# Summing the last states in pairs, and moving the convolution, the last product and the first statistics, in a four-stage block on one core

## The reference

```
x = x + attention(layernorm(x))   # RMS norm with norm_w gives xn; 16 heads of 16, causal softmax; returns xn + out @ Wo.T + bo
x = x + ffn(layernorm(x))         # base product + shared and 6 routed rank-16 adapters, top 2 of 6 by softmax of a router
x = x + ssm(layernorm(x))         # below
x = x + ffn(layernorm(x))         # the same weights again

xc    = silu(causal depthwise convolution of 4 taps + conv_b)
delta = softplus(xc @ Wd.T + bd);  B = xc @ Wb.T;  C = xc @ Wc.T        # 16 states n
h_n[t] = exp(A_n * delta[t]) * h_n[t-1] + delta[t] * xc[t] * B_n[t]
y[t]   = sum over n of h_n[t] * C_n[t]
return (y * sigmoid(x @ Wg.T + bg)) @ Wo.T + bo
```

## Time and profile before

| | |
|---|---|
| time, median of 3 runs | 2346.57 us (2340.99 to 2353.04) |
| the profiled execution's own time | 2343.07 us |
| its span, first to last instruction | 2341.3 us |
| mean granted clock of TensorE | 0.901 |
| TensorE busy | 1801.8 us, 77% |
| VectorE busy | 1820.6 us, 78% |
| ScalarE busy | 1292.8 us, 55% |
| GpSimd busy | 1061.9 us, 45% |
| accumulates y<-hc | 240 of 512 KB, median 6.1 us from issue to landing |
| loads of a row of B | 256 of 256 KB, median 3.7 us |
| load of one batch of x | 16 of 512 KB, median 5.3 us |

### The profile page before, as it was taken

One profiled execution on the slowest core, in us unless ns is written; L12 is line 12 of the kernel. 1 busy time (PEld: TensorE's weight loads), 2 busy tenths in 40 slices (PEclk: granted clock), 3 DMA queues, 4 the chain that ended last, 5 costly groups with the idle time before them and its releaser, 6 DMA issues. The chain is left out here.

```text
span 2341.3 us, 31537 instructions
## 1 busy us (share of the span) xinstructions
PE 1801.8 (77%) x10784; PEld 1088.8 (47%) x10784; DVE 1820.6 (78%) x2791; ACT 1292.8 (55%) x2258; POOL 1061.9 (45%) x672
## 2 busy tenths in 40 slices
PE   3789887878788787878888797878878797866433
PEld 1445444545364454536454454635445453534222
DVE  4444878879797888969797878979787887959693
ACT  1455656565756556565656556565655655554331
POOL 1010544636354545535464543545454553546461
PEclk8899899999999899999999899999999998986756
DMA  3211565747665665756566674766557574645462
GB/s 108 78 55 60 122 144 123 166 106 167 127 134 124 131 150 126 161 111 146 123 132 143 127 161 106 165 120 145 122 123 157 118 159 101 137 93 123 95 143 45
DMA packets 190370, 291.25 MB, mean 124 GB/s; under 512 B 34034, under 2 KB 126211, under 8 KB 190211
## 3 DMA queue, kind: packets, MB, share of 16 engines
q1 hardware_dynamic: 155650, 163.40, 28.5%
q0 software_dynamic: 34560, 125.84, 28.1%
HBM read 128.72 MB, written 34.08 MB: 70 GB/s over the span
## 5 line engine op out<-in xcount | busy, mean ns | idle before, releaser
L1174 POOL TENSOR_TENSOR inp<-u,b_all 128x1024 f32<-128x1024 f32 x256 | 608.0, 2375 | 638.8 <-DVE hc L1027 517.4
L1027 DVE TENSOR_TENSOR_SCAN hc<-dec,inp 128x1024 f32<-128x1024 f32 x256 | 644.0, 2516 | 4.1 <-ACT dec L796 3.0
L707 ACT ACTIVATE pt<-bank 128x512 f32<-128x512 f32 x640 | 382.8, 600 | 410.3 <-PE bank L340 406.6
L315 PE MATMUL bank<-sk,sq 96*128 96x512 bf16 (+3 forms) x1024 | 283.7, 316 | 204.8 <-DVE mall L914 64.5
L796 ACT ACTIVATE dec<-dt,a_neg 128x511 f32<-128x511 f32 x512 | 338.5, 721 | 72.6 <-DVE hc L1027 72.5
L1182 POOL DMA_DIRECT2D y<-hc x240 | 211.6, 882 | 316.8 <-DVE hc L1034 183.6
L1034 DVE TENSOR_TENSOR hc<-hc,bank 128x1024 f32<-128x1024 f32 x240 | 291.1, 1213 | 61.3 <-PE bank L486 60.0
L338 PE MATMUL bank<-sq,sk 98*128 98x512 bf16 (+3 forms) x1024 | 280.6, 313 | 29.9 <-DMA sq<-hlt 21.0
L912 DVE TENSOR_REDUCE mall<-bank 128x1 f32<-128x512 f32 x256 | 171.6, 670 | 111.2 <-PE bank L317 111.1
L315 PEld LDWEIGHTS bank<-sk,sq 96*128 96x128 bf16 x1024 | 102.6, 100 | 330.8 <-DVE mall L914 86.3
L914 DVE TENSOR_REDUCE mall<-bank 128x4 f32<-128x512 f32 x256 | 174.8, 683 | 37.9 <-PE bank L317 33.7
(11 more groups left out here) (148 smaller groups left out, 3186.5 us busy)
## 6 DMA issues: line engine op xcount, KB each, us to landing
y<-hc POOLq DMA_DIRECT2D x240, 512.0 KB, 6.1
b_all<-b_kept SPq DMA_DIRECT2D x256, 256.0 KB, 3.7
qk_parts<-parts SPq DMA_DIRECT2D x96, 256.0 KB, 2.5
sq<-qk_parts SPq DMA_DIRECT2D x384, 64.0 KB, 4.1
sk<-qk_parts SPq DMA_DIRECT2D x384, 64.0 KB, 4.3
X<-in_x SPq DMA_DIRECT2D x16, 512.0 KB, 5.3
out<-X SPq DMA_DIRECT2D x16, 512.0 KB, 4.5
sq<-hlt SPq DMA_DIRECT2D x256, 2.0 KB
```

The costliest lines, as they stand in the source:

```text
L315: mm(dst[:, o:o + n], sq[0:KS, slot, h, qb * P:(qb + 1) * P], sk[0:KS, slot, h, 0:n], start=True, stop=False)
L707: A(pt[:, n % PT, :], score_bank[unit % 2][:, :], ACT.Exp).then_inc(exp_done.sem, 1)
L1027: V.tensor_tensor_scan(h, d, v, 0.0, ALU.mult, ALU.add).then_inc(scan_done.sem, 1)
L1174: G.tensor_tensor(inp[:, n % 2, :, :], u[:, :, :], b_all[:, n % 2:n % 2 + 1, :].to_broadcast([P, C, T]), ALU.mult).then_inc(inp_ready.sem, 1)
```

## The change

- **Pairs.** For batches 14 and 15 (`PAIRED = NB - 2`), after the product of an even state n = 2, 4, ..., 14 VectorE adds the slot of n - 1 to that of n, and one DMA adds the sum to y. State 15 is added alone. These batches have 8 accumulates each instead of 15, counted by `pair_added`; a scan waits for `pair_done` where its slot held an odd state, and for `pair_added` where it held an even one.
- **Convolution ahead of the gates.** Both halves of the convolution are at (3, 0), in banks MA and MB, both gates at (3, 1), in the same banks.
- **Last product a position later.** `gate_y` goes from (0, 1) to (0, 2), behind the scan of that position; `ssm_out` from (0, 4) to (0, 5); adding to X from (0, 4) to (0, 5) and the statistics to (0, 6); `rsqrt` from (0, 4) to (0, 7); normalising from (0, 9) to (1, 0). `turn_xn` goes from (0, 6) to (0, 3), and `head_norm` from the end of position 4 to position 5, behind the maximum and ahead of the scan.
- **Three slots for B.** Load k goes into slot k % 3 and waits for the inp of k - 3; the first three loads of a batch are issued together at (3, 4).
- **Start.** The statistics of the first x come first on VectorE, behind one small memset; the other memsets and the fold into Wv go into `constants`; Wv moves from the first to the other weights. ScalarE does one small exp ahead of its loop and waits for the constants at q = -1.
- The router's scratch tile `over` is dropped; `diff` is overwritten.

```diff
+    PAIRED = NB - 2
-        b_all = sb("b_all", [P, 2, T])
+        b_all = sb("b_all", [P, 3, T])
-    N_FIRST, N_REST = 5, 21
+    N_FIRST, N_REST = 4, 22
...
+            def ssm_conv(f, c):
+                m = (MA, MB)[c]
+                pe.wait_ge(m.free, m.fill(("conv", f, c)))
...
             def ssm_gate(f, c):
+                m = (MA, MB)[c]
+                pe.wait_ge(m.free, m.fill(("gate", f, c)))
+                by_columns(m.tile, wg, xs_t[:, :, TAPS - 1:], c).then_inc(m.full, 1)
...
-                    if (r, p, j) == (0, 6, 0):
+                    if (r, p, j) == (0, 3, 0):
                         turn_xn(b + 1)
...
-                    elif r == 3 and p in (0, 1):
-                        if j == 0:
-                            ssm_gate(f, p)
-                        else:
-                            ssm_conv(f, p)
+                    elif (r, p) == (3, 0):
+                        ssm_conv(f, j)
+                    elif (r, p) == (3, 1):
+                        ssm_gate(f, j)
...
-                    if (r, p) == (0, 4):
+                    if (r, p) == (0, 5):
                         ssm_out(l, j)
...
+                    old_s, old_n = divmod(k - 3, NS)
+                    sp.wait_ge(inp_ready.sem, inp_ready.at(old_s, old_n + 1))
+                    if n < 3:
                         sp.wait_ge(b_stored.sem, b_stored.at(s))
+                    sp.dma_start(b_all[:, k % 3, :], b_kept[s, n][None, :].to_broadcast([P, T])
+                                 ).then_inc(b_loaded[k % 3].sem, 16)
...
-                    if (r, p, j) == (0, 9, 0):
+                    if (r, p, j) == (1, 0, 0):
                         normalise(l, KIND_L, X[:, l % XS, :, :], y_tok(l))
...
+            act.wait_ge(pool_const, 1)
+            A(ex[:, 0, 0:1], ident[:, 0:1], ACT.Exp)
...
-                if q == -3:
+                if q == -1:
                     act.wait_ge(dve_const, 1)
...
+                    if old_n == 0:
+                        dve.wait_ge(hc_done.sem, hc_done.at(old_s, 1))
+                    elif old_s < PAIRED:
                         dve.wait_ge(y_added.sem, y_added.at(old_s, old_n))
+                    elif old_n % 2 and old_n < NS - 1:
+                        dve.wait_ge(pair_done.sem, pair_done.at(old_s - PAIRED, old_n // 2 + 1))
                     else:
+                        dve.wait_ge(pair_added.sem, pair_added.at(old_s - PAIRED, (old_n + 1) // 2))
...
+                    if s >= PAIRED and n and n % 2 == 0:
+                        dve.wait_ge(hc_done.sem, hc_done.at(s, n + 1))
+                        V.tensor_tensor(hc[:, k % HC, :, :], hc[:, k % HC, :, :], hc[:, (k - 1) % HC, :, :],
+                                        ALU.add).then_inc(pair_done.sem, 1)
...
-                    if (r, p) == (0, 1):
+                    if (r, p) == (0, 2):
                         gate_y(l)
-                    elif (r, p) == (0, 4):
+                    elif (r, p) == (0, 5):
                         add_to_x(l, ("x3",), (MA, MB))
+                    elif (r, p) == (0, 6):
                         moments(l, KIND_L, 1.0, 1e-5)
...
             V.memset(half[:, :], -0.5)
+            dve.wait_ge(x_loaded.sem, x_loaded.at(0))
+            moments(0, KIND_Q, 1.0 + 1e-6, 1e-5 * 1e-6)
             dve.wait_ge(pool_const, 1)
...
+                    if p == 5 and 0 <= q - 1 < NQ:
+                        head_norm(q - 1)
                     if p in STEP_AT:
                         scan(k + STEP_AT[p])
                     if p in PRODUCT_AT:
                         product(k + PRODUCT_AT[p])
-                    if p == 4 and 0 <= q - 1 < NQ:
-                        head_norm(q - 1)
...
+            def add_pair(s, n):
+                if n % 2 == 0:
+                    pool.wait_ge(pair_done.sem, pair_done.at(s - PAIRED, n // 2))
+                else:
+                    pool.wait_ge(hc_done.sem, hc_done.at(s))
+                if n > 2:
+                    pool.wait_ge(pair_added.sem, pair_added.at(s - PAIRED, (n - 1) // 2))
+                pool.dma_start(y[:, s % 2, :, :], hc[:, (NS * s + n) % HC, :, :],
+                               accum_op=ALU.add).then_inc(pair_added.sem, 16)
...
-                    elif (r, p) == (0, 4) and has(b - 3):
+                    elif (r, p) == (0, 7) and has(b - 3):
                         rsqrt(b - 3, KIND_L)
```

More of the change, by code:

```diff
@@ L245, in hybrid_block @@
         b_stored = tally("b_stored", 1, 16)
-        b_loaded = [tally(f"b_loaded{i}", NS // 2, 16) for i in range(2)]
+        b_loaded = [tally(f"b_loaded{i}", 1, 16) for i in range(3)]
         c_ready = tally("c_spread", NS)
@@ L448, in ssm_turn @@
                     turn(tok_f, m.tile, c).then_inc(m.full, 1)
-            def ssm_gate(f, c):
[L451 to L461, removed]
+            def ssm_conv(f, c):
+                m = (MA, MB)[c]
+                pe.wait_ge(m.free, m.fill(("conv", f, c)))
+                for k in range(TAPS):
+                    last = mm(m.tile[:, :], taps[:, c, k, :], xs_t[:, c, k:k + T], start=(k == 0),
+                              stop=(k == TAPS - 1))
+                last.then_inc(m.full, 1)
+            def ssm_gate(f, c):
+                m = (MA, MB)[c]
+                pe.wait_ge(m.free, m.fill(("gate", f, c)))
+                by_columns(m.tile, wg, xs_t[:, :, TAPS - 1:], c).then_inc(m.full, 1)
             def ssm_bc(f):
@@ L686, in _ @@
                         store_b(b - 1)
-                        load_b(NS * (b - 1))
-                        load_b(NS * (b - 1) + 1)
+                        for n in range(3):
+                            load_b(NS * (b - 1) + n)
                     if (r, p) == (3, 9) and has(b + 1):
                         store_parts(b + 1, 1)
-                    if (r, p) == (3, 9) and has(b - 1):
-                        load_b(NS * (b - 1) + 2)
             sp.wait_ge(x_stored.sem, x_stored.at(NB - 1))
@@ L757, in sigmoid_gate @@
             def sigmoid_gate(f, c):
-                act.wait_ge(MA.full, MA.at("gate", f, c))
-                A(gate[:, f % 2, c, :], MA.tile[:, :], ACT.Tanh, bias=bg_c[:, c:c + 1], scale=0.5).then_inc(MA.free, 1)
+                m = (MA, MB)[c]
+                act.wait_ge(m.full, m.at("gate", f, c))
+                A(gate[:, f % 2, c, :], m.tile[:, :], ACT.Tanh, bias=bg_c[:, c:c + 1], scale=0.5).then_inc(m.free, 1)
             def convolved(f, c):
-                act.wait_ge(MB.full, MB.at("conv", f, c))
-                A(sp_t[:, c, :], MB.tile[:, :], ACT.Tanh, bias=cb[:, c:c + 1])
-                A(xc[:, c, :], MB.tile[:, :], ACT.Identity, bias=cb[:, c:c + 1]).then_inc(MB.free, 1)
+                m = (MA, MB)[c]
+                act.wait_ge(m.full, m.at("conv", f, c))
+                A(sp_t[:, c, :], m.tile[:, :], ACT.Tanh, bias=cb[:, c:c + 1])
+                A(xc[:, c, :], m.tile[:, :], ACT.Identity, bias=cb[:, c:c + 1]).then_inc(m.free, 1)
             def bc_high(f):
@@ L838, in after_attention @@
                         copy_turned(("xs",), f, xs_t[:, :, TAPS - 1:])
[L839 to L843, removed]
+                    elif (r, p) == (3, 0):
+                        convolved(f, j)
+                    elif (r, p) == (3, 1):
+                        sigmoid_gate(f, j)
                     elif (r, p) == (3, 3):
@@ L1042, in constants @@
             def constants():
+                V.memset(xc[0:3 * NC, :, :].rearrange("p c t -> p (c t)")[:, 3 * D:3 * D + LR - E], 0.0)
+                V.memset(pick[:, :], 0.0).then_inc(dve_own.sem, 1)
+                dve.wait_ge(dve_own.sem, dve_own.one())
+                for j in range(3):
+                    V.memset(pick[j * NC:j * NC + 1, :], 1.0)
+                V.memset(v_sb[:, :, :], 1.0)
+                V.memset(sk[KS:KS + 2, :, :, :], 1.0)
+                V.memset(dec[:, :, :, :], 0.0)
+                V.memset(xs_t[:, :, 0:TAPS - 1], 0.0)
+                V.memset(wts[:, :, :], 1.0)
+                V.memset(hw[:, :, :, ER:], 1.0).then_inc(dve_own.sem, 1)
+                dve.wait_ge(dve_own.sem, dve_own.one())
                 dve.wait_ge(w_rest, 16 * N_REST)
-                dve.wait_ge(act_const, 1)
-                V.tensor_scalar(a_neg[:, :, :], a_neg[:, :, :], -1.0, None, ALU.mult)
+                for c in range(C):
+                    V.tensor_scalar(wv[:, c, :], wv[:, c, :], w_col[:, c:c + 1], None, ALU.mult)
                 V.tensor_scalar(bg_c[:, :], bg_c[:, :], 0.5, None, ALU.mult)
@@ L1143, in _ @@
                     after_ssm(b - 3, r, p)
-                    if (r, p) == (2, 9) and has(b + 2):
+                    if (r, p) == (2, 9) and has(b + 2) and b + 2 > 0:
                         dve.wait_ge(x_loaded.sem, x_loaded.at(b + 2))
@@ L1188, in after_step @@
                     inputs(s, n + 2)
-                if has(s) and n:
+                if has(s) and n and s < PAIRED:
                     add_state(s, n)
+                elif has(s) and n and (n % 2 == 0 or n == NS - 1):
```

(1 more changed line is left out.)

44 lines of the change are left out of this document (17 added, 27 removed).

## The result

| kernel | median, us | runs | ratio to before, 95% |
|---|---|---|---|
| before | 2344.61 | 2340.99 to 2353.04 | |
| after | 2283.32 | 2281.89 to 2291.34 | 0.9741 [0.9705, 0.9776] |

Faster by 61.3 us in the medians. (The median of before has one run more than the 2346.57 us given ahead of the prediction.) Predicted were 2289 and a range of 2258 to 2328. The profiled execution of after took 2291.34 us (span 2289.6), the slowest of its four; between the two profiled executions lie 51.7 us. In the page of after, TensorE is busy 1788.5 us, VectorE 1833.3, and there are 226 accumulates into y instead of 240.

What follows compares the result with a forecast made beforehand. VectorE and TensorE's interlock bound 370 to 1980 us; VectorE, GpSimd and the accumulate chain the tail. -7 - 43 - 5 - 30 + 17 + 10 = -58 gave 2285 profiled, median 2289, range 2258 to 2328.

Steps and rivals of the forecast that it cites:

- late statistics: Later rsqrt and normalising of L delay the spread matmul: 1.2 us per batch, 17 given back; bounds 0 to about 7.
- third slot: GpSimd's waits for B, 33.1 us in 13 times: a gain of 0, bounds -1 to +1 us per batch.
- y quarter: The r = 0 quarter, later gating, product and heads: 3.3 us per batch, 43 in all, plus 5 in batches 13 and 14.
- convolution first: Both convolutions ahead of the gates let silu start earlier: 1.9 us per batch, 16 times, 30 us.
- pairs: Batches 14 and 15: sums wait for inp, then delay the next scan; +6.3 and +3.5, together 10 us slower.
- start: Kernel start: first projection begins at 17.9 instead of 24.87, a gain of 7 us, bounds 0 to 11.
- Gating one position later: Maximum and scan ahead of the gating fill its wait for y's last accumulate: 2.8 us per batch, bounds 0 to 5.0.
- new wait for X: In the r = 0 quarter, VectorE waits for the product's second half before adding X: 1.0 us, bounds 0 to 2.5.
- rival 2: Slower: the chain of L holds up spread and maxima; break-even 5.4 us per batch, 2369 at 7; chance 0.06.
- tail steps with a sum that take no longer: Sign against the forecast: in batches 14 and 15, steps with a pair sum last no longer than those without.
- Rival 1: VectorE's removed waits reappear at the score matmuls; 2326 if half of 73 steady us stays; chance 0.20.
- Rival 4: The reorder does nothing for the gating, as the accumulate lands later: 2331; chance 0.05.

Runs made afterwards that it cites:

- e4: The kernel after with the statistics of L and their rsqrt at position 5 and the normalising at (0,9): 2224.16 us, ratio 0.9504.
- e13: The kernel before with the later gating, product, heads and turned xn, but statistics of L and rsqrt at position 5, normalising at (0,9): 2278.71 us, ratio 0.9711.
- e2: The kernel after with its r = 0 quarter (gating, product, heads, turned xn, statistics, normalising) back at the old places: 2265.42 us, ratio 0.9685.
- e7: The kernel before with both convolutions ahead of the gates and nothing else: 2309.07 us, ratio 0.9835.
- e3: The kernel after with gates and convolution back in their old alternating order: 2311.47 us, ratio 0.9875.
- e9: The kernel before with three slots for B and the scratch tile dropped, nothing else: 2303.74 us, ratio 0.9818.
- e6: The kernel after with two slots for B, loaded as before: 2306.10 us, ratio 0.9812.
- e1: The kernel after without pair sums, each state of batches 14 and 15 added by its own DMA: 2278.41 us, ratio 0.9731.

## Why the prediction came out right, and where it was wrong

The total came out within 6 us of the forecast, and that was luck. The price of the late statistics was 39 us too low; against it stood 17 to 43 us for the third slot, which the sum had at nothing, and up to 20 for the y quarter. In us, measured as ratios times 2345:

| part | predicted | alone in before | taken out of after (or e4) |
|---|---|---|---|
| y quarter without late statistics | -48 | -68 (e13) | -42 (e2 to e4) |
| late statistics of L | +17 | +56 | +56 (e4) |
| convolution first | -30 | -39 (e7) | -31 (e3) |
| third slot for B | 0 | -43 (e9) | -17 (e6) |
| pairs | +10 | not run | +2, unclear (e1); +5.4 in the trace, the end's 2 taken off |
| start | -7 | not run | trace only: -6.5 |
| sum | -58 | -99 with the last two as found | -39 |

- *Start: right.* Copies of the turned x end and the first projection starts at 17.34 (predicted 17.9, before 24.87); the first score matmul for a maximum comes at 39.20, before at 45.67.
- *Gating one position later: right, and low.* y's wait is 1.3 us in all. Alone, with early statistics (e13), the quarter gives 5.3 us per batch, not 3.3: the heads' wait went in full, and the new wait for X that I charged with 1.0 is 1.07 per batch in all in after, against 0.64 before.
- *Price of the later statistics: wrong, the step that failed.* I followed GpSimd's chain to the next spread matmul and compared it with the slack of products 4 and 5, which indeed don't wait in the batch shown. The chain was about right: the spread came 9.1 us behind the end of scan 3 in after (median of 13 batches), and 5.2 in e4 and 5.5 in before, so 3.7 to 3.9 us later, against the 2.5 that I worked out in a batch in which TensorE was slow already. Wrong was to end there and to set slack against it. Behind TensorE's turn stand the FFN of the batch, the router and the maxima, and the delay reaches the router on VectorE nearly whole: 19.8 us behind scan 3 against 16.1 in e4. 4.0 us per batch, not 1.2. My bound of 7 held it. This is rival 2's mechanism, at less than its break-even of 5.4.
- *Three slots: wrong, 0 instead of 17 to 43.* I asked only whether VectorE waits for inp. It doesn't; but inp feeds the accumulates, and SP's late loads of B share its queue with what TensorE waits for (the parts of each were not separated). Row 6's 33.1 us were not idle time without a cost, and my bounds of 1 us per batch were too narrow.
- *Convolution: right* (1.9 per batch; 2.1 measured alone, 1.6 in after), silu's wait gone.
- *Pairs: right in mechanism, high in size.* Sums start at the product's end, take until inp has ended and then 1.22; the last two are 10.43 us apart (10.6 predicted). This is what the Trainium skill states (SBUF — State Buffer, "Who interferes with whom"), and the trace agrees, 2.29 against 1.22. But batch 14 paid 3.8 instead of 6.3, and batch 15 1.6 instead of 3.5, since without pairs its steps are 5.1 us apart and not much faster. So my sign "tail steps with a sum that take no longer" nearly came, 10.43 against 10.2 us for two, and not because the sum hides.
- *Rival 1, the interlock,* is real between the edits. The singles add to 99 us where 61 came, and taken out one by one they add to 39. Each is worth less with the others there (slots 43 and 17, y quarter 68 and 42; convolution 39 and 31, which the noise doesn't tell apart). The third slot gains 1.0 per batch at the gating, which has little to gain when it is later: with two slots (e6) it waits for y 2.0 us in all.
- *Rival 4* (the gating gains nothing) fell with the wait for y. Not tested was how the quarter's 5.3 us divide among gating, heads and product, nor the start by itself.

## What to carry to other kernels

A right total of many terms says little about the terms: take each large edit out, and put it in alone. When a step is moved later, follow every engine's queue behind it to the next place where the bounding engines meet, through two hand-overs and not one, and add the work that TensorE does at its lower clock behind a new idle stretch. A wait of a side engine for a load is no free slack until what it feeds, and what stands behind the load in the same queue, has been followed too.

## What the runs showed of the hardware

- TensorE's granted clock fell to 0.51 for 5 us behind 4.4 us with two matmuls in them (1292.69 + 1.07 to 1298.16), and the same eight transposes took 1.97 instead of 1.04 us. So an idle wait of 2.64 us cost more than itself on TensorE. In the middle batch of before, a wait of 1.98 us for a DMA (clock 1.00 from 1327.90 to 1329.95) was followed by a clock of 0.52 for 3.45 us.
- The gating, two SBUF tiles in, takes 1.19 us free. Three of 16 in after took 2.9 to 3.3, none in before or in e2, where it stands one position earlier: at its new place it can meet inp on GpSimd. It is the sums' case again, and each time about 2 us.
